# A routing list summed from upper and lower parts, with GpSimd making the token parts

## What is computed

```python
scores = softmax(xt @ gate_w.T)                 # 2048 tokens, 16 experts
masked = scores in the best 2 of 4 groups       # else 0
w, eidx = top_k(masked, 4); w = w / w.sum()
for e in range(16):                             # 4 choices a token carry weight
    out += cw[:, e:e+1] * (swiglu(xt @ expert_up_w[e].T) @ expert_down_w[e].T)
out += swiglu(xt @ shared_up_w.T) @ shared_down_w.T
```

## Time and profile before

| | |
|---|---|
| median of 3 runs | 1859.88 us (1859.28 to 1862.43) |
| the profiled execution | 1859.53 us, its span 1857.7 us |
| granted TensorE clock, mean | 0.944 |
| busy: PE, DVE, ACT, POOL | 88%, 78%, 44%, 57% of the span |
| `mamba` | about 0 to 1126 us |
| `shared` | about 1128 to 1347 us |
| `experts` | about 1348 us to the end |

### The profile page before, as it was taken

One profiled execution on the slowest core, in us unless ns is written; L12 is line 12 of the kernel. 1 busy time (PEld: TensorE's weight loads), 2 busy tenths in 40 slices (PEclk: granted clock), 3 DMA queues, 4 the chain that ended last, 5 costly groups with the idle time before them and its releaser, 6 DMA issues. The chain is left out here.

```text
span 1857.7 us, 28398 instructions
## 1 busy us (share of the span) xinstructions
PE 1641.9 (88%) x7884; PEld 1200.2 (65%) x7884; DVE 1453.7 (78%) x1945; ACT 819.4 (44%) x1220; POOL 1062.5 (57%) x832
## 2 busy tenths in 40 slices
PE   8667867898997988887778999999989999999998
PEld 5255434555455655455454647778889999999997
DVE  3599999999999999999999933877455566565654
ACT  2656666566766567665655411000022233232322
POOL 0289579887599795797987671000044444344443
PEclk9868879999998999999978999999989999999999
DMA  5112212223323222331223243111156665666664
GB/s 129 36 59 69 59 40 72 66 80 97 68 86 108 80 80 80 91 98 57 74 65 119 84 153 124 68 69 52 54 141 151 161 164 135 169 137 146 151 176 70
DMA packets 130022, 181.92 MB, mean 98 GB/s; under 512 B 21443, under 2 KB 79555, under 8 KB 126788
## 3 DMA queue, kind: packets, MB, share of 16 engines
q1 hardware_dynamic: 109540, 131.85, 22.2%
q0 software_dynamic: 17888, 43.79, 12.1%
q10 hardware_dynamic: 2432, 4.33, 0.9%
HBM read 276.18 MB, written 37.36 MB: 169 GB/s over the span
## 5 line engine op out<-in xcount | busy, mean ns | idle before, releaser
L1194 POOL TENSOR_TENSOR arena_kept<-arena_kept,b_all 128x512 f32<-128x512 f32 x512 | 637.4, 1275 | 250.6 <-DVE arena_kept L1078 124.2
L1078 DVE TENSOR_TENSOR_SCAN arena_kept<-da,arena_kept 128x512 f32<-128x512 f32 x512 | 598.0, 1205 | 12.9 <-ACT da L927 9.4
L927 ACT ACTIVATE da<-arena_kept,a_neg 128x504 f32<-128x504 f32 x512 | 347.5, 684 | 245.6 <-DVE arena_kept L1078 239.4
L716 PE MATMUL hT<-ident_kept,arena_kept 128*128 128x128 f32 x2048 | 314.7, 301 | 143.8 <-DVE yacc L1090 89.3
L716 PEld LDWEIGHTS hT<-ident_kept,arena_kept 128*128 128x128 f32 x2048 | 257.4, 155 | 247.1 <-DVE arena_kept L1078 171.4
L1090 DVE SCALAR_TENSOR_TENSOR yacc<-hT,c_now,yacc 128x512 f32<-128x512 f32 x480 | 331.6, 733 | 4.6 <-PE hT L716 4.3
L2107 POOL DMA_INDIRECT out<-y,slots_kept x76 | 134.8, 1773 | 233.1 <-issue 174.4
L516 PE MATMUL bank<-hid,wt 128*128 128x512 f32 x512 | 239.1, 615 | 0.9 <-ACT hid L752 0.7
L516 PEld LDWEIGHTS bank<-hid,wt 128*128 128x128 f32 x512 | 98.6, 201 | 107.2 <-issue 105.1
L1977 ACT ACTIVATE gs<-egp 128x352 f32<-128x352 f32 x73 | 33.9, 464 | 238.3 <-PE eup L1287 237.7
L1739 POOL DMA_DIRECT2D slots_kept<-lists_kept x1 | 0.6, 567 | 212.3 <-DVE lists_kept L1691 212.3
(11 more groups left out here) (235 smaller groups left out, 3160.6 us busy)
## 6 DMA issues: line engine op xcount, KB each, us to landing
w_up_kept<-in_up_T SPq DMA_DIRECT2D x76, 1408.0 KB, 5.9
w_dn_kept<-in_dn_T SPq DMA_DIRECT2D x76, 768.0 KB, 7.2
b_all<-bt_scratch SPq DMA_DIRECT2D x128, 256.0 KB, 3.5
wt<-in_in_T SPq DMA_DIRECT2D x64, 256.0 KB, 3.0
wt<-in_out_T SPq DMA_DIRECT2D x32, 256.0 KB, 2.9
res<-in_x_pad SPq DMA_DIRECT2D x16, 256.0 KB, 3.7
x_scratch<-res SPq DMA_DIRECT2D x16, 256.0 KB, 2.2
wt<-in_w_T SPq DMA_DIRECT2D x16, 256.0 KB, 3.1
```

Source lines behind the costliest of these rows:

```text
L716: mm = nc.tensor.transpose(turned_in(j, m, t)[:, d * P:(d + 1) * P], h[:, m % RING, d, t * P:(t + 1) * P], ident[:])
L927: nc.scalar.activation(out[:, :, 1:], rows[:, :, 1:], ACT.Exp, scale=a_neg[:, d, n:n + 1]) \
L1078: nc.vector.tensor_tensor_scan(h[:, n % RING, i, :], da[i % RING][:], dbx[:, i, :], 0.0, ALU.mult, ALU.add).then_inc(scan_done, 1)
L1194: nc.gpsimd.tensor_tensor(dbx[:, i, :], u[:, d, :], b_all[:, m % RING, :], ALU.mult) \
```

## The change

Chunks become half as large (4 choices) and twice as many (16), and a step handles two of them (AT_ONCE = 2). TensorE sums in step s what was made in step s - 1 (BEHIND = 2). Token and weight are split once into upper and lower parts (4 more `slots` steps of 64 elements). Of each chunk VectorE makes the two products with the weight's parts, and GpSimd the two with the token's parts; all are fp32r, as is `at_row`. A matmul of the sum has 340 moving columns in fp32r in place of 170 in fp32. `at_tile` has one buffer, so VectorE waits ahead of writing it for the products of the chunk before on both engines (`picks_made`, `tokens_made`); TensorE waits for both as well. `list_out` adds the two halves (4 instructions in place of 2) and comes at s = 10. The zeros of the padding rows lie in another tile.

```diff
-PICKS = TILES * TOP // 8
+PICKS = TILES * TOP // 16
+AT_ONCE = 2
 CHUNKS = TILES * TOP // PICKS
 FIRST_PICK = 1
-BEHIND = FIRST_PICK + 2
+BEHIND = FIRST_PICK + 1
...
-    at_row = sb("at_row", [P, RING, PICKS, P])
+    value_hi = [sb(f"value_hi{v}", [P, TILES, TOP], F32R) for v in range(2)]
+    value_lo = [sb(f"value_lo{v}", [P, TILES, TOP], F32R) for v in range(2)]
+    at_row = sb("at_row", [P, RING, PICKS, P], F32R)
...
-    to_list = sb("to_list", [P, RING, PICKS, 2, LIST_TILES])
+    to_list = sb("to_list", [P, RING, PICKS, 4, LIST_TILES], F32R)
...
             def sum_picks(c):
                 pe.wait_ge(picks_made, 3 * (c + 1))
+                pe.wait_ge(tokens_made, 2 * (c + 1))
                 for i in range(PICKS):
-                    mm = nc.tensor.matmul(list_ps, at_row[:, c % RING, i, :],
+                    mm = nc.tensor.matmul(list_ps[:].rearrange("p a b -> p (a b)")[:, 0:4 * LIST_TILES], at_row[:, c % RING, i, :],
                                           to_list[:, c % RING, i].rearrange("p v n -> p (v n)"),
...
-                    if 0 <= (j - 2) * KS + f - BEHIND < CHUNKS:
-                        sum_picks((j - 2) * KS + f - BEHIND)
+                    if 0 <= (j - 2) * KS + f - BEHIND < CHUNKS // AT_ONCE:
+                        for c in range(AT_ONCE):
+                            sum_picks(AT_ONCE * ((j - 2) * KS + f - BEHIND) + c)
...
-                    if 0 <= (j - 2) * KS + f - FIRST_PICK < CHUNKS:
-                        picks((j - 2) * KS + f - FIRST_PICK)
-                    if (j - 2) * KS + f == CHUNKS + BEHIND:
+                    if 0 <= (j - 2) * KS + f - FIRST_PICK < CHUNKS // AT_ONCE:
+                        for c in range(AT_ONCE):
+                            picks(AT_ONCE * ((j - 2) * KS + f - FIRST_PICK) + c)
+                    if (j - 2) * KS + f == CHUNKS // AT_ONCE + BEHIND:
                         list_out()
...
+                for v, value in enumerate((token, weight)):
+                    yield step(hi_part(nc.vector, value_hi[v][:], value[:]))
+                    yield step(lo_part(nc.vector, value_lo[v][:], value[:], value_hi[v][:]))
...
-                step(nc.vector.tensor_tensor(at_tile, list_numbers[:].unsqueeze(1).broadcast_to(by_list),
-                                             mine(of_tile[:]).unsqueeze(2).broadcast_to(by_list), ALU.is_equal))
-                for v, value in enumerate((token, weight)):
+                if c:
+                    dve.wait_ge(tokens_made, 2 * c)
+                    dve.wait_ge(picks_made, 3 * c)
+                nc.vector.tensor_tensor(at_tile, list_numbers[:].unsqueeze(1).broadcast_to(by_list),
+                                        mine(of_tile[:], c).unsqueeze(2).broadcast_to(by_list), ALU.is_equal).then_inc(tile_found, 1)
+                dve.wait_ge(tile_found, c + 1)
+                for v, value in ((2, value_hi[1]), (3, value_lo[1])):
                     nc.vector.tensor_tensor(to_list[:, c % RING, :, v, :], at_tile,
-                                            mine(value[:]).unsqueeze(2).broadcast_to(by_list), ALU.mult).then_inc(picks_made, 1)
+                                            mine(value[:].bitcast(F32), c).unsqueeze(2).broadcast_to(by_list), ALU.mult) \
+                        .then_inc(picks_made, 1)
...
+            pool.wait_ge(pads_stored, 32)
+            for c in range(CHUNKS):
+                pool.wait_ge(tile_found, c + 1)
+                if c >= RING:
+                    pool.wait_ge(picks_summed, c - RING + 1)
+                for v, value in ((0, value_hi[0]), (1, value_lo[0])):
+                    nc.gpsimd.tensor_tensor(to_list[:, c % RING, :, v, :], at_tile,
+                                            mine(value[:].bitcast(F32), c).unsqueeze(2).broadcast_to(by_list), ALU.mult) \
+                        .then_inc(tokens_made, 1)
+
             pool.wait_ge(listed, 2)
-            pool.wait_ge(pads_stored, 32)
```

More of the change, by code:

```diff
@@ L1395, in shared @@
     list_numbers = sb("list_numbers", [P, LIST_TILES])
+    list_sum = sb("list_sum", [P, 2, LIST_TILES])
     strict = sb("strict", [P, P])
@@ L1424, in shared @@
     t_tmp = sb("t_tmp", [1, LIST_TILES])
-    pad_rows = to_list[:, 0].rearrange("p i v n -> p (i v n)")[:, 0:DM]
+    pad_rows = keep["xg"][:, 0, :]
     gp = [ps(f"gp{i}", [P, BLK]) for i in range(RING)]
@@ L1430, in shared @@
     yp = [ps(f"yp{i}", [P, DM]) for i in range(RING)]
-    within = ps("within", [P, TILES, EXP])
+    list_ps = ps("list_sums", [P, 4, P])
+    within = list_ps[:, 0:2, :].rearrange("p a b -> p (a b)").rearrange("p (t e) -> p t e", t=TILES)
     totals = ps("totals", [P, TILES, EXP])
@@ L1452, in shared @@
     picks_made = sem("picks_made")
+    tile_found = sem("tile_found")
+    tokens_made = sem("tokens_made")
     picks_summed = sem("picks_summed")
@@ L1459, in shared, with mine @@
     ahead_in = sem("ahead_in")
+    by_list = [P, PICKS, LIST_TILES]
+    def mine(x, c):
+        return x.rearrange("p t k -> p (t k)")[:, c * PICKS:(c + 1) * PICKS]
     x1_blk = x1_d.rearrange("(k t p) f -> k p t f", t=TB, p=P)
     out_blk = out_d[0:TOK].rearrange("(k t p) f -> k p t f", t=TB, p=P)
-    list_ps = within[:].rearrange("p t e -> p (t e)")[:, 0:2 * LIST_TILES]
+    sums = [list_ps[:].rearrange("p a b -> p (a b)")[:, v * LIST_TILES:(v + 1) * LIST_TILES] for v in range(4)]
     N_CONST = 7
@@ L1553, in counts @@
                 pe.wait_ge(keep["rank_step"], RANKS)
-                nc.tensor.matmul(within[:], strict[:], sel[:], start=True, stop=True).then_inc(counts_full, 1)
+                nc.tensor.matmul(within, strict[:], sel[:], start=True, stop=True).then_inc(counts_full, 1)
                 nc.tensor.matmul(totals[:], ones[:], sel[:], start=True, stop=True).then_inc(counts_full, 1)
@@ L1643, in slots @@
                 yield step(nc.vector.tensor_tensor(starts[:], ends[:], tiles[:], ALU.subtract))
-                yield step(nc.vector.tensor_tensor(place[:], within[:], before[:].rearrange("p e t -> p t e"), ALU.add))
+                yield step(nc.vector.tensor_tensor(place[:], within, before[:].rearrange("p e t -> p t e"), ALU.add))
                 yield step(nc.vector.scalar_tensor_tensor(out=place[:], in0=starts[:].unsqueeze(1).broadcast_to([P, TILES, EXP]),
@@ L1667, in picks @@
             def picks(c):
-                def mine(x):
-                    return x.rearrange("p t k -> p (t k)")[:, c * PICKS:(c + 1) * PICKS]
-                by_list = [P, PICKS, LIST_TILES]
                 if c == 0:
@@ L1677, in picks @@
                 nc.vector.tensor_tensor(at_row[:, c % RING], row_numbers[:].unsqueeze(1).broadcast_to([P, PICKS, P]),
-                                        mine(in_tile[:]).unsqueeze(2).broadcast_to([P, PICKS, P]), ALU.is_equal) \
+                                        mine(in_tile[:], c).unsqueeze(2).broadcast_to([P, PICKS, P]), ALU.is_equal) \
                     .then_inc(picks_made, 1)
-                step(nc.vector.tensor_tensor(at_tile, list_numbers[:].unsqueeze(1).broadcast_to(by_list),
-                                             mine(of_tile[:]).unsqueeze(2).broadcast_to(by_list), ALU.is_equal))
-                for v, value in enumerate((token, weight)):
+                if c:
[5 more added lines that the diff above has]
+                for v, value in ((2, value_hi[1]), (3, value_lo[1])):
                     nc.vector.tensor_tensor(to_list[:, c % RING, :, v, :], at_tile,
-                                            mine(value[:]).unsqueeze(2).broadcast_to(by_list), ALU.mult).then_inc(picks_made, 1)
+                                            mine(value[:].bitcast(F32), c).unsqueeze(2).broadcast_to(by_list), ALU.mult) \
+                        .then_inc(picks_made, 1)
             def list_out():
@@ L1689, in list_out @@
                 lists = keep["lists"]
-                nc.vector.tensor_scalar(lists[:, :, 0], list_ps[:, 0:LIST_TILES], pad_row_f[:, 0:1], None, ALU.add).then_inc(listed, 1)
-                nc.vector.tensor_copy(lists[:, :, 1].bitcast(F32), list_ps[:, LIST_TILES:]).then_inc(listed, 1)
+                step(nc.vector.tensor_scalar(list_sum[:, 0, :], sums[0], pad_row_f[:, 0:1], None, ALU.add))
+                step(nc.vector.tensor_copy(list_sum[:, 1, :], sums[2]))
+                nc.vector.tensor_tensor(lists[:, :, 0], list_sum[:, 0, :], sums[1], ALU.add).then_inc(listed, 1)
+                nc.vector.tensor_tensor(lists[:, :, 1].bitcast(F32), list_sum[:, 1, :], sums[3], ALU.add).then_inc(listed, 1)
             def slot_tiles():
```

## The result

The changed kernel takes 1868.04 us (median of 5 runs, 1866.29 to 1870.64), the kernel before 1859.28 us beside it (5 runs, 1855.45 to 1862.43): ratio 1.0049, interval 1.0034 to 1.0063, so 8.8 us slower.

A forecast was written before the change was run, and what follows sets the result against it. TensorE was taken as the bound, to be replaced by VectorE and GpSimd together. Block 3 begins 11.1 us late, nothing changes in it, and 2 us go to the clock: +13 us, 1873.0 us on the median, range 1864 to 1885 us.

The forecast's parts named there:

- the sign: The whole kernel becomes slower, +13 us; chance of slower 0.83, of faster 0.08.
- the GpSimd product: GpSimd's two-input product of 340 elements in each chunk was claimed to take 0.91 us.
- a full step: From one VectorE multiplication to the next, with two chunks: 8.05 us, against TensorE's 6.68.
- The sum: Blocks 2 and 3 together get longer by 11.1 us, before anything for the granted clock.
- The blocks: Block 2 makes block 3 begin 11.1 us late; within block 3 waits and sums of 11.9 us equal today's sums.
- The third down tile of block 2: TensorE waits there for VectorE's first addition, which comes 11.6 us later; costs another 2.5 us.
- The clock: TensorE's granted clock falls after its stops in blocks 2 and 3: none to 5 us, 2 taken.
- five singles and three pairs: TensorE's stops in blocks 2 and 3: three pairs (1.0 to 1.25 and 2.9 us), five single ones of 1.4 to 2.5.
- A: Rival: VectorE and GpSimd do not exclude each other on these instructions; -0.7, 1859 us; chance 0.12.
- B: Rival: the token parts are ready in time, so only TensorE's saving stays; -9.1, 1850.8 us; chance 0.06.
- C: Rival: GpSimd's products take as long as those of 512 elements; +23, 1885 us; chance 0.20 with sizes down to the forecast.
- The bounds of the GpSimd product alone: GpSimd's product of 340 takes between 0.83 and 1.275 us, which gives +9 to +23 us.

The follow-up runs named there:

- e6: The kernel before, with the change's four values made by VectorE alone, chunks of 8, summed two steps behind, GpSimd idle: 1858.07 us, ratio 0.9988.
- e1: The changed kernel, but VectorE makes all four products of a chunk and GpSimd none: 1866.02 us, ratio 1.0030.
- e3: The changed kernel with four buffers for to_list and TensorE summing two steps behind (BEHIND = 3), GpSimd's part unchanged: 1863.93 us, ratio 1.0016.
- e4: The kernel before with fp32r sums of 340 columns, lower parts left out as zeros written once: 1851.95 us, ratio 0.9955.
- e2: The changed kernel without VectorE's two products of a chunk, the weight's parts being zeros written once: 1858.22 us, ratio 0.9997.

## Why the prediction was right, and where it was off

**Right: the sign and what carries it.** TensorE was the bound and lost that place to VectorE and GpSimd together. They exclude each other as the long row of the scans had shown; e10 shows it by moving one input of VectorE's products to PSUM. Products at the shapes of this change were stretched from 0.51 to 1.06. TensorE waits where it was said to, in pairs at steps 2, 5 and 7 (0.7 and about 2.2 each time; forecast 1.0 to 1.25 and 2.9), for GpSimd's products, through 9 waits and 10.9 us. What the prediction does not name is the price of the plan: by the ruler of e6, e1 and the change, the half-size chunks and the shorter distance cost 6.4 us and GpSimd's part 1.8.

**Off in size: the GpSimd product.** The step that failed is "2.1 ns an element and 0.2 fixed, so 0.91 us for 340". It was 0.75. The three rows do not lie on a line with a fixed part: 1408 and 1536 elements are 2.24 ns each, 340 elements 2.2, and the rows of 512, taken beside the scans, are 0.1 above that. I read this surplus as a start-up cost. The estimate of 0.71 by the Trainium skill's GPSIMD Engine Reference (Instruction dispatch), which I set aside, was nearer. With 0.75 in the same account a full step is 1.79 + 0.60 + 0.53 + 2.62 + 0.54 + 1.49 = 7.57 us against 8.05; measured 7.46. The sum becomes +7.1 instead of +11.1, against +8.1 by the ruler.

**The blocks.** Block 2 came 9.8 late, forecast 11.1; block 3 won 1.8, forecast 0.1, as a shorter step makes them (8.7 late and 1.6 won in the same account with 0.75). The third down tile of block 2 waited 0.3, not 2.5, and that is not the shorter step's doing: with 0.75 the account still has TensorE 6.5 late into the down products and the addition's end 8.7 late, a wait of 2.2. TensorE was 8.0 late there and lost more time behind it, to the clock.

**The clock.** It fell twice, behind the two pairs in block 2 (granted clock in stretches of 2 us):

```profile
1252.00:1254.00 2.00, 2.00 (x6) 1.58 (x5) 1.97 (x4) 0.00 (x0) 1.28 (x2) 0.50 0.00 0
...
1276.00:1278.00 2.00, 2.00 (x6) 1.52 (x6) 1.97 (x4) 0.00 (x0) 1.35 (x2) 0.50 0.00 0
```

Each fall took some 1.7 us of products. Here the forecast's picture was incomplete: the lost time did not only shorten TensorE's next wait (none at step 3, where 1.4 was forecast). The first fall made VectorE wait for the slowed products, its only wait from step 1 to the first addition of block 2:

```profile
1258.67 0.69 DVE L1611 TENSOR_TENSOR sa<-sgs,up 128x512 f32<-128x512 f32 x1 [1.39 <-PE up L1287]
```

In e3, where the clock did not fall before the down products, this wait is missing and the first addition comes 1.4 us sooner after block 1's store (52.8 against 54.2 us). So the first fall cost about 1.4 us, and the second was hidden ahead of the third down tile. 7.1 and 1.4 make 8.5, against 8.1 by the ruler; the forecast had 2 for the clock. In block 3 the stops of 0.7 and 2.2 us brought no fall, so the count of five singles and three pairs said little.

**The rivals.** A (no exclusion, -0.7) fell with e10. B (-9.1) fell with the changed kernel's own trace, its 9 waits at the sums and products of 0.75, not 0.5. C, a longer product, was the wrong way. The bounds of the GpSimd product alone gave +9 to +23; the +8.1 of the ruler and the 8.8 of the medians lie just below, because the lower bound of 0.83 was above the true 0.75. The stated range held because it reached down to 1864, to the slower part of rival A. That is partly luck.

## What to carry to other kernels

Look at where the inputs lie before handing work from VectorE to GpSimd: here, with both inputs of VectorE's instructions in SBUF, each engine waited for the other and a step took 7.46 us with GpSimd's help and 7.47 without it. Before more is put behind steps on a full engine, look for its idle time elsewhere in the plan: here moving the same work between the additions was worth 7 to 8 us, more than the cheaper sums' 5.6. And a producer moved closer to its consumer is priced where the consumer has little else to do or the producer starts late, here behind the 12 products of step 5, and at steps 2 and 7, after VectorE's late start behind the slot steps and the table. Halving the pieces to make this fit has a price of its own, here 0.5 us a step.

## What was not expected of the hardware

- GpSimd's two-input instruction has no fixed part to see between 340 and 1536 elements: 0.75, 3.15 and 3.43 us, 2.2 ns an element.
- The recorded duration of a GpSimd or VectorE instruction holds its wait for the other: 1.08 recorded, 0.75 alone. Durations from a busy stretch are no price.
- fp32r matmuls of 256 columns follow each other every 0.12 us with a new stationary operand each.
- A single wait of TensorE of 1.24 us (e4) had the lower clock behind it, while six waits of 6.2 us together in e2, the longest 1.5, and the pair of 0.66 and 2.24 us in block 3 of the changed kernel had not.
